# A fused Perceiver kernel: in two cross attentions the exponentials are issued one round later and the values are copied by VectorE

## The reference

```python
q = x_norm @ Wq            # 32 rows, 16 heads of 8
k = ctx @ Wk               # 257 rows
v = ctx @ Wv
p = softmax(q k^T * 8 ** -0.5, over the 257 rows)
x = x + (p v) @ Wo + bo
```

## Time and profile before

| what | value |
|---|---|
| median of 3 runs | 3848.38 us (3839.97 to 3863.2) |
| the profiled execution | 3855.02 us, of which the profile's span is 3853.3 us |
| PE / DVE / ACT / POOL busy in the span | 81% / 52% / 34% / 18% |
| granted TensorE clock, mean | 0.907 of full |
| instructions | 64884 |

### The profile page before, as it was taken

One profiled execution on the slowest core, in us unless ns is written; L12 is line 12 of the kernel. 1 busy time (PEld: TensorE's weight loads), 2 busy tenths in 40 slices (PEclk: granted clock), 3 DMA queues, 4 the chain that ended last, 5 costly groups with the idle time before them and its releaser, 6 DMA issues. The chain is left out here.

```text
span 3853.3 us, 64884 instructions
## 1 busy us (share of the span) xinstructions
PE 3123.1 (81%) x23914; PEld 2009.6 (52%) x23914; DVE 2005.9 (52%) x6137; ACT 1323.1 (34%) x3783; POOL 695.0 (18%) x1501
## 2 busy tenths in 40 slices
PE   6999978776967776987677776554799999999799
PEld 5888865554445554655435554333444444444365
DVE  4888875555044446659864445654323232323444
ACT  1444433332245652235366555442111111111222
POOL 1333420000045550023104444010000000000000
PEclk8999998988989997987789998786899999999899
DMA  3010000000011100120021100003100000000100
GB/s 88 24 26 25 24 16 1 1 1 4 1 45 32 34 22 19 29 66 1 15 54 36 28 26 23 1 1 108 62 1 1 1 1 1 1 1 1 37 1 12
DMA packets 164818, 83.62 MB, mean 22 GB/s; under 512 B 78803, under 2 KB 158678, under 8 KB 164310
## 3 DMA queue, kind: packets, MB, share of 16 engines
q1 hardware_dynamic: 164502, 79.47, 8.0%
HBM read 75.75 MB, written 3.67 MB: 21 GB/s over the span
## 5 line engine op out<-in xcount | busy, mean ns | idle before, releaser
L3068 PE MATMUL bank<-WhhT,hT 128*64 128x512 f32 (+1 forms) x4096 | 681.4, 488 | 29.5 <-ACT hT L3131 29.5
L3068 PEld LDWEIGHTS bank<-WhhT,hT 128*64 128x64 f32 x4096 | 285.8, 137 | 374.1 <-issue 256.4
L1005 ACT ACTIVATE probs<-probs,nbias 128x257 f32<-128x257 f32 x512 | 254.4, 499 | 285.5 <-DVE nbias L1093 283.8
L1182 POOL TENSOR_SCALAR probs<-probs,rinv 128x257 f32<-128x257 f32 x512 | 236.8, 482 | 256.7 <-DVE rinv L1099 256.6
L3245 POOL COPY rb<-hT 128x512 f32<-128x512 f32 x32 | 35.7, 1117 | 922.8 <-ACT hT L3131 901.5
L3220 DVE TENSOR_TENSOR pr<-hb,bank 128x512 f32<-128x512 f32 x32 | 22.0, 688 | 343.1 <-PE bank L3110 343.1
L729 POOL TENSOR_SCALAR probs<-probs,rinv 128x257 f32<-128x257 f32 x256 | 120.1, 482 | 278.0 <-DVE rinv L667 278.0
L925 PE MATMUL bank<-ident,probs 128*128 128x128 f32 x1024 | 155.4, 300 | 0.0
L551 ACT ACTIVATE probs<-bank,nbias 128x257 f32<-128x257 f32 x256 | 119.3, 471 | 81.7 <-DVE rinv L667 71.0
L477 PE MATMUL bank<-kvT,qh 128*128 128x257 f32 x512 | 136.9, 391 | 4.6 <-ACT kvT L542 4.6
L925 PEld LDWEIGHTS bank<-ident,probs 128*128 128x128 f32 x1024 | 122.8, 153 | 30.0 <-issue 29.7
(11 more groups left out here) (658 smaller groups left out, 6814.4 us busy)
## 6 DMA issues: line engine op xcount, KB each, us to landing
kvT<-in_ctx_T SPq DMA_DIRECT2D x128, 128.5 KB
raw<-in_L_ffn_gru_w_hh SPq DMA_DIRECT2D x24, 512.0 KB, 4.5
kv<-in_ctx SPq DMA_DIRECT2D x64, 128.0 KB
kv<-in_ctx SPq DMA_DIRECT2D x32, 256.0 KB
W<-in_L_ffn_W SPq DMA_DIRECT2D x64, 64.0 KB, 2.2
v_last<-v_last SPq DMA_DIRECT2D x192, 8.0 KB, 1.6
mask_u<-in_mask_BxSxS_bk SPq DMA_DIRECT2D x64, 32.1 KB, 2.0
mask_u<-in_mask_Bx1xSxS_bf SPq DMA_DIRECT2D x64, 32.1 KB, 2.0
```

The costliest lines, as they stand in the source:

```text
L1005: i = e.activation(s, s, ACT.Exp, bias=self.nbias[v][:, r:r + 1], scale=self.scale, accum_out=self.rows_sum[v][:, r:r + 1])
L1182: e.tensor_scalar(s, s, self.rinv[v][:, r:r + 1], 1.0, ALU.mult, ALU.mult)
L3068: mm = e.matmul(self.bank[b][hf * BATCH:(hf + 1) * BATCH, 0:n], lhs, rhs, start=start, stop=stop, tile_position=(0, hf * BATCH))
```

## The change

It has four parts, all in this class:

- ACT: the copy of the values goes away; the exponentials are issued one round later (`g + 2` in round g).
- DVE: a new `copy_values` copies the values of batch g + 4 out of the shared bank as the first thing of round g, after ACT's key copy (it waits for `k_ready`). `inverses` is moved ahead of `row_maxes`, and is that of batch g + 1 in place of g + 2.
- POOL: `normalise` is that of batch g + 1 in place of g + 2.
- The starts of the loops (the first rounds) are fitted to that. PE's code is unchanged.

```diff
@@ act
             if g + 4 < BATCH:
                 self.copy_keys_values(e, g + 4)
-            if g + 3 < BATCH:
-                self.exponentials(e, g + 3)
+            if g + 2 < BATCH:
+                self.exponentials(e, g + 2)
...
         i.then_inc(self.k_ready.up(), 1)
-        self.attended.wait_ge(e, g - self.V_RING + 1)
-        e.copy(self.v[g % self.V_RING][:, :], x[:, 2 * P:4 * P]).then_inc(self.v_ready.up(), 1)
@@ dve
         for g in range(BATCH):
             t, b = g // BPT, g % BPT
+            if g + 4 < BATCH:
+                self.copy_values(e, g + 4)
             if b == 0 and t + 1 < NT:
                 self.take_queries(e, t + 1)
             if b == 1 and t:
                 self.spread_last(e, t - 1)
             if b == 2 and t:
                 self.add_bo(e, t - 1)
+            if g + 1 < BATCH:
+                self.inverses(e, g + 1)
             if g + 3 < BATCH:
                 self.row_maxes(e, g + 3)
-            if g + 2 < BATCH:
-                self.inverses(e, g + 2)
             if g + 1 < BATCH:
                 self.copy_pT0(e, g + 1)
...
+    def copy_values(self, e, g):
+        self.k_ready.wait_ge(e, g + 1)
+        self.attended.wait_ge(e, g - self.V_RING + 1)
+        e.tensor_copy(self.v[g % self.V_RING][:, :], self.bank[self.X_BANK][:, 2 * P:4 * P]).then_inc(self.v_ready.up(), 1)
@@ pool
-            if g + 2 < BATCH:
-                self.normalise(e, g + 2)
+            if g + 1 < BATCH:
+                self.normalise(e, g + 1)
```

More of the change, by code:

```diff
@@ L970, in act @@
             self.copy_keys_values(e, g)
-            if g:
-                self.exponentials(e, g - 1)
+            if g > 1:
+                self.exponentials(e, g - 2)
         self.copy_pT1(e, 0)
@@ L1044, in dve @@
         for g in range(3):
+            self.copy_values(e, g)
             self.row_maxes(e, g)
-            if g:
-                self.inverses(e, g - 1)
+            if g == 1:
+                self.inverses(e, 0)
+        self.copy_values(e, 3)
         self.copy_pT0(e, 0)
@@ L1137, in pool @@
             self.put_k_last(e, g)
-            if g > 1:
-                self.normalise(e, g - 2)
+        self.normalise(e, 0)
         for g in range(BATCH):
```

## The result

The changed kernel took 4045.06 us (median of 4, 4041.78 to 4048.3) beside 3851.03 us for the kernel before on the same chips: a ratio of 1.0503, 95% interval 1.0469 to 1.0537. It is slower by 194 us. The forecast was slower by 130 us, 3978 us with a range from 3930 to 4040. The direction and the loop were right; the size was not, and the time lies outside the range.

What follows compares the result with a forecast made beforehand. No engine is full; a loop of waits through ACT's exponentials and `nbias` sets the pace. New loop 31.2 + 32.4, clock 45.9 and edges 20 sum to +130 us: 3985 profiled, 3978 median, range 3930 to 4040.

Steps and rivals of the forecast that it cites:

- the loop: Serial chain each round: transposes, keys and values, `kT`, `v`, any small product, `rinv`, `normalise`, transposes; +31.2 and +32.4 us.
- `v` to `turn_last` at position 1: Hop from DVE's values copy to PE's small product in a tile's round at position 1: 0.47 us.
- `v` on DVE: The values copy out of PSUM, moved to DVE: taken as 0.425 us, bounds 0.29 to 0.58.
- the position sums: Full-clock lengths of a tile's four rounds, positions 0 to 3: 6.81, 5.67, 6.91 and 5.01 us.
- The clock term: PE's work on the new loop at half pace in low-clock time, granted clock 0.85: 1.64 us a tile, +45.9.
- The bound on the clock: Granted clock from 0.92 to 0.75 in the two stages: -22 to +33 us against the value at 0.85.
- the signals: Signals between engines, taken as 0.05 us; at 0.09, twice a round, they would add 10 us.
- The edges: First tile and last three rounds of a stage, longer by 5.1 and 5.0 us: +20 for two stages.
- Start of the stages: Start before the first transposes, fewer ACT copies and a later first exponential: costed at 0, between -2 and +3.
- The clock gives way more: Rival: same loop, longer PE waits lower the clock to 0.75; 4011 us, up to 4040; chance 0.15.
- Normalise stays out of the loop: Rival: `rinv` made before the keys and values of g + 4, so POOL is hidden; about 3660 us; chance 0.03.
- the old loop: Kernel before: serial waits through ACT's exponentials, `kT`, `v`, small product, row maxima and `nbias`; 5.57 us at position 1.

Runs made afterwards that it cites:

- experiment 3: Changed kernel with inverses of batch g + 1 ahead of DVE's values copy and its normalising ahead of POOL's spread and mask mapping: 3725.03 us, 0.9678 of the kernel before.
- experiment 4: Changed kernel with only the inverses of batch g + 1 moved ahead of DVE's values copy, POOL's order kept: 3835.15 us, 0.9968 of the kernel before.
- experiment 7: Changed kernel with fewer filler transposes (10, 5, 5, 2) and POOL normalising only two of four parts of a batch: 3831.93 us.
- experiment 1: Also called `fill`: changed kernel, PE filling its wait for normalised probabilities with identity transposes (20, 14, 14, 10): 3942.14 us, 1.0248 of the kernel before.
- experiment 2: Kernel before the change, with filler transposes (7, 16, 17, 0) in PE's wait for the values: 3848.63 us, 0.9995 of the kernel before.
- the two best kernels: Changed kernel with inverses and normalising of batch g + 1 moved first, 3725.03 us; the same with the values copy back on ACT, 3708.84 us.

## Why the prediction was wrong in size and right in kind

- **The loop was right.** Each hop at full clock came out within 0.1 us (the largest miss is `v` to `turn_last` at position 1, 0.57 for 0.47): `v` on DVE 0.424 in the stage (0.425 taken), the position sums 6.77, 5.75, 6.91 and 4.99 in the shortest rounds against 6.81, 5.67, 6.91 and 5.01. Against the old tiles as measured, the full-clock loop costs (24.43 - 22.17 + 24.90 - 22.53) x 14 = 65 us; the forecast had 31.2 + 32.4 = 64. Experiments 3, 4 and 7 show that it is this loop.
- **The clock term failed.** "26 x 0.30 x 0.42 / 2 = 1.64 per tile, +45.9 for 28" is 93.2 measured by experiment 1, so 47 of the missing 61 us. Two parts of the step were wrong. The first is the value 0.85, taken as the nearest row of the kernel before: layer 1 got 0.86, but layer 3 0.81 on average, lower than any tile of it had shown. With the clocks measured and the old weight the term would have been 54 us, so this is some 8 of the 47. The second is the weight, the other 39. I multiplied the time at the low level with PE's share of the loop at full clock. In that time PE's part is doubled, so its share is 2 x 0.42 / (1 + 0.42) = 0.59, and half of that is lost: 0.30 of each low microsecond and not 0.21. Measured it was 3.74 us for 28.17 x 0.38 = 10.7 low us in layer 3, 0.35; and 2.92 for 27.82 x 0.28 = 7.8 in layer 1, 0.37. The rest, 0.05 to 0.07, is there because the low time does not fall evenly over the round. The low level sets in near the start of the burst behind the wait: in all 61 cases of the steady tiles between 1.7 us before and 1.4 us after the start of the transposes. In layer 3 PE is busy for 90% of the low time and for 68% of all time, and 3.3 of the 3.74 us fall on the first two hops (experiment 1). Nor is the weight a constant of the kernel's own: from experiment 2 it was 0.25 and 0.19 in the two stages of the kernel before (7.95 us lost in 31.5 low ones, 9.48 in 49.7), near my 0.21. I take it that less of PE's work in the low time lay on that loop; no run shows this.
- **The bound on the clock failed with it.** Its far end, 0.75, was priced by the same formula at 2.84 us a tile; the true cost at 0.81 was already 3.74. So the range ended 5 us short. The bounds of the prediction, all high, came to 4046, and the stated range left these last 6 us out. That it came so near is luck: the clock's term was 14 us too low even at its far end (2.84 x 28 = 79.5 against 93.2), and the room given to `v` and to the signals, which they did not use, made up for most of that.
- **The edges** were 28 us against 20. At full clock, in `fill`, first tiles and tails were 22.5 longer. The rest is the clock there, less what filler costs: it made the tail of layer 1 longer, 13.25 in place of 12.53. Start of the stages and all else: 5 us, costed at 0.
- **The rivals.** "The clock gives way more" was what happened in kind, with its price too small: the clock was 0.86 and 0.81, not as low as its 0.75, and the time was still above its 4011 and its 4040. "Normalise stays out of the loop" did not happen but decides the matter, as experiment 3 shows: the forecast gave it some 3660 us, the kernel in which it holds took 3725 and 3709. In that rival I had given no time to PE, which is busy for 86 to 91% of the tiles there.

## What to carry to other kernels

When an operation is moved a round later, follow its result to the next consumer, and ask of each queue on the way which waiting instruction now stands ahead of it: here one that had been a round early was put behind the shared bank, and the fix was two lines of order. When a loop passes through PE more than once, price the TensorE clock as part of it: here low time cost 0.35 to 0.37 of itself, more than PE's share of the loop at the low level gives (0.30), since it fell on the burst behind each wait. If the change adds waits, the bound should be taken from a lower clock than any that the old trace shows. And a filler kernel separates loop and clock in one run, where PE has a wait to fill.

## What the runs showed of the hardware

- Filler transposes that write a bank about to be overwritten held the granted clock of both stages at 1.00 and took 103 us off a kernel whose useful work was unchanged. In the kernel before, the same gave nothing net (0.9995), since what it brought the steady tiles it cost at the edges.
- Layer 3 of the changed kernel, with PE waits of 1.6 to 2.8 us in all but one round of the steady tiles, ran at a granted 0.81; in the two best kernels, whose longest wait for POOL is 1.2 us in layer 3 and 1.5 in layer 1, and in which some rounds have none, the steady tiles ran at 1.00. The 0.81 cost 3.7 us a tile, more than the lengthened loop itself (2.9 against the old loop at full clock).
- Between `fill` and the changed kernel only the hops that hold work of PE differ; the three kinds without it agree to 0.01 us a tile. At the low level a burst's transposes took 1.76 us to the next product, at the full one 0.93.
- VectorE and GpSimd beside one another did not slow GpSimd here to speak of: the normalising instruction took 485 ns in the changed kernel, where it overlaps the row maxima, and 482 before.
